# The expert phase of an attention and mixture-of-experts kernel: two tiles at a time instead of one

## What is computed

```python
x = x + xattn(layernorm(x), ctx, ctx, Wq, Wk, Wv, Wo, bo, mask)   # 32 batches x 256 tokens x 256, 16 heads of 64, causal
x = x + ffn(layernorm(x), router_w, router_b, weights1, bias1, weights2, bias2)

def ffn(x, ...):
    logits = x_flat @ router_w.T + router_b          # 8192 tokens, 32 experts
    routed_idx = argmax(logits)
    h = relu(x_flat @ w1[e] + b1[e])                 # 256 -> 64
    y = relu(h @ w2[e] + b2[e])                      # 64 -> 256
    # each token takes the y of its own expert
```

## Time and profile before

| what | us |
|---|---|
| median of 3 runs | 1811.64 (1810.61 to 1812.76) |
| the profiled execution, own time | 1811.58 |
| its span, first to last instruction | 1809.8 |
| TensorE busy in the span | 1753.6 |
| VectorE, ScalarE, POOL busy | 1247.4, 1033.9, 282.4 |

### The profile page before, as it was taken

One profiled execution on the slowest core, in us unless ns is written; L12 is line 12 of the kernel. 1 busy time (PEld: TensorE's weight loads), 2 busy tenths in 40 slices (PEclk: granted clock), 3 DMA queues, 4 the chain that ended last, 5 costly groups with the idle time before them and its releaser, 6 DMA issues. The chain is left out here.

```text
span 1809.8 us, 42548 instructions
## 1 busy us (share of the span) xinstructions
PE 1753.6 (97%) x12580; PEld 1356.3 (75%) x12581; DVE 1247.4 (69%) x5361; ACT 1033.9 (57%) x3206; POOL 282.4 (16%) x377
## 2 busy tenths in 40 slices
PE   5999999999999999999999999999999996899997
PEld 4777788778877887777877788788778874566664
DVE  5677777777777777777777777777777776233332
ACT  4656666666666666666666666666666663343442
POOL 1011011111111111111111111111101111233333
PEclk9999999999999999999999999999999998555555
DMA  7830000000000000000000000000000000333321
GB/s 209 237 99 21 24 24 24 22 21 24 24 24 24 24 24 24 24 24 24 20 22 24 24 24 24 24 24 24 24 24 18 18 12 16 90 101 101 86 70 24
DMA packets 70009, 77.61 MB, mean 43 GB/s; under 512 B 11703, under 2 KB 64093, under 8 KB 69985
## 3 DMA queue, kind: packets, MB, share of 16 engines
q1 hardware_dynamic: 61778, 60.18, 11.9%
q0 software_dynamic: 7680, 16.93, 2.6%
q10 hardware_dynamic: 528, 0.22, 0.0%
HBM read 47.60 MB, written 33.88 MB: 45 GB/s over the span
## 5 line engine op out<-in xcount | busy, mean ns | idle before, releaser
L672 ACT ACTIVATE Sm<-Sm,mneg 128x128 f32<-128x128 f32 (+1 forms) x1024 | 455.5, 448 | 366.9 <-DVE mneg L904 366.1
L904 DVE CUSTOM_DVE_ANT_0 Sm<-psS,MK 128x128 f32<-128x128 f32 (+1 forms) x1024 | 304.4, 353 | 123.7 <-PE psS L519 114.0
L546 PE MATMUL psO<-PT,V 128*64 128x256 f32 x2048 | 277.5, 392 | 2.3 <-ACT PT L665 2.0
L519 PE MATMUL psS<-KT,QT 64*128 64x128 f32 (+1 forms) x2048 | 238.5, 351 | 4.4 <-DVE mneg L904 2.6
L530 PEld LDWEIGHTS psT<-ident,Sm 128*128 128x128 f32 x1536 | 163.7, 141 | 98.7 <-issue 98.1
L530 PE MATMUL psT<-ident,Sm 128*128 128x128 f32 x1536 | 224.6, 282 | 0.0
L546 PEld LDWEIGHTS psO<-PT,V 128*64 128x64 f32 x2048 | 124.3, 136 | 123.8 <-issue 74.6
L665 ACT ACTIVATE PT<-psT 128x768 f32<-128x768 f32 x256 | 205.5, 803 | 6.6 <-PE psT L530 2.5
L672 ACT ACTIVATION_READ_ACCUMULATOR Sm<-Sm,mneg 128x1 f32 x1024 | 195.1, 191 | 0.0
L921 DVE TENSOR_TENSOR Sm<-Sm,rinv 128x512 f32<-128x512 f32 x256 | 192.8, 753 | 0.0
L519 PEld LDWEIGHTS psS<-KT,QT 64*128 64x128 f32 x2048 | 134.9, 187 | 59.7 <-issue 44.3
(11 more groups left out here) (151 smaller groups left out, 3229.8 us busy)
## 6 DMA issues: line engine op xcount, KB each, us to landing
lists<-pad SPq DMA_DIRECT2D x8, 1560.0 KB, 16.4
XS<-lists SPq DMA_DIRECT2D x96, 130.0 KB, 2.1
x_in<-in_x SPq DMA_DIRECT2D x32, 256.0 KB, 2.7
ctx_in<-in_ctx SPq DMA_DIRECT2D x32, 256.0 KB, 2.7
xr<-in_x SPq DMA_DIRECT2D x32, 256.0 KB, 2.7
W2R<-in_L_ffn_weights SPq DMA_DIRECT2D x1, 2048.0 KB
out<-Y,tok POOLq DMA_INDIRECT x96, 2.6
W2R<-in_L_xattn_Wq SPq DMA_DIRECT2D x1, 1024.0 KB, 10.1
```

Of the source, the lines that this page charges most:

```text
L519: last = nc.tensor.matmul(psS[:, side, o:o + (it + 1) * P], QT[rows, p, it * P:(it + 1) * P], KT[rows, p, 0:(it + 1) * P], start=True, sto ...
L546: last = nc.tensor.matmul(psO[DH * side:DH * side + DH, 0:N], V[:, t, DH * h:DH * h + DH], PT[:, side, cols], start=(t == 0), stop=(t == 1))
L672: nc.scalar.activation(v, v, ACT.Exp, bias=mneg[:, p % 2, k:k + 1], scale=-1.0, accum_out=rsum[:, p % 2, k:k + 1]).then_inc(s_exp, 1)
L904: nc.vector.tensor_tensor_reduce(out=Sm[:, p % 4, side, cols], in0=psS[:, side, cols], in1=MK[:, cols], scale=-SCALE, scalar=3e38, op0=ALU ...
```

## The change

The expert phase works on pairs of tiles. There are `NP` = 48 pairs (`NET` stays 96) and eight buffers for pairs. One load brings both tiles. The buffers, PSUM tiles and semaphore steps hold a pair: four transposes, then the W1 products of the two tiles alternately, one into PSUM partitions 0 to 63 and one into 64 to 127, then two W2 products. VectorE normalises twice and adds once per pair; ScalarE copies W1 for the first tile of the pair and VectorE for the second. The bias comes from a table `B1T`, transposed twice over (so `b1` is loaded into two halves), and is no longer a column of `W1R`; the ReLU is one instruction for each tile, with an index load of its own. SyncE waits with the next load of a buffer for the addition that has read it (`s_y`), not for the stores; VectorE waits for the stores of the buffer's last use before it writes `tok` and `Y` anew. The token numbers are copied at the addition, not at the norm. On VectorE the memsets of `HT` come after the table row.

```diff
-    NET = -(-(NT + E - 1) // U) * U
+    NP = B * N // P // 2 + E // 2
+    NET = 2 * NP
...
-            act.dma_start(b1_in[:], b1).then_inc(s_small, 16)
+            for half in range(2):
+                act.dma_start(b1_in[:, half, :], b1).then_inc(s_small, 16)
...
-            nc.vector.memset(W1R[HID:P, :, KD * HID], 0.0)
             dve.wait_ge(s_b1_pe, 1)
-            nc.vector.tensor_copy(W1R[0:HID, :, KD * HID], psS[0:HID, 1, 0:E]).then_inc(s_b1r, 1)
+            nc.vector.tensor_copy(B1T[:], psS[:, 1, 0:E]).then_inc(s_b1r, 1)
...
-        psXT = [psS[:, u, :] for u in range(2)]
-        psH = [psT[:, u, :] for u in range(2)]
-        psY = [psO, psW]
+        psXT = [psO, psW]
+        psH = psR
+        psY = [psS, psT]
...
+                        for t in range(2):
+                            nc.gpsimd.indirect_dma_start(out_rows, bass.IndirectOffsetOnAxis(ap=tok[u][:, t:t + 1], axis=0),
+                                                         Y[u][:, t, :], None, bounds_check=last_token, oob_is_err=False
+                                                         ).then_inc(s_done[u], 16)
...
-                        wait_apart(sp, s_passed, s_done[u], 16 * i)
+                        wait_apart(sp, s_passed, s_y, U * (i - 1) + u + 1)
                         load(i, u)
...
+                def norm_pair(i, u):
                     dve.wait_ge(s_in[u], 16 * i + 16)
+                    for t in range(2):
+                        last = nc.vector.tensor_scalar(XH[u][:, t, :], XS[u][:, t, 0:D], XS[u][:, t, D:D + 1],
+                                                       XS[u][:, t, D + 1:D + 2], ALU.subtract, ALU.mult)
+                    last.then_inc(s_xh, 1)
+
+                def add_pair(i, u, free):
+
+                    if free:
+                        wait_apart(dve, s_passed, s_done[u], 32 * i)
+                    nc.vector.tensor_copy(tok[u][:], XS[u][:, :, D + 2])
                     dve.wait_ge(s_y_pe, U * i + u + 1)
+                    nc.vector.scalar_tensor_tensor(out=Y[u][:], in0=psY[u % 2][:, :, 0:D], scalar=0.0,
+                                                   in1=XS[u][:, :, 0:D], op0=ALU.max, op1=ALU.add).then_inc(s_y, 1)
+
+                def w1_copy(i, u):
+                    e = expert(dve, U * i + u, 1)
+                    nc.vector.tensor_copy(W1[u][:, 1, :], W1R[:, bass.ds(e, 1), :].rearrange("p a c -> p (a c)")
+                                          ).then_inc(s_w1[1], 1)
...
                 def hidden(i, u):
+                    e = [expert(act, U * i + u, t) for t in range(2)]
                     act.wait_ge(s_h_pe, U * i + u + 1)
+                    for t in range(2):
+                        last = nc.scalar.activation(HT[u][0:HID, t, :], psH[u % 2][half(t), 0:P], ACT.Relu,
+                                                    bias=B1T[half(t), bass.ds(e[t], 1)])
+                    last.then_inc(s_h, 1)
...
                     for c in range(KD):
-                        last = nc.tensor.matmul(psH[u % 2][0:HID, 0:P], W1[u][:, c * HID:(c + 1) * HID],
-                                                XHT[u][:, c, :], start=(c == 0), stop=(c == KD - 1))
+                        for t in range(2):
+                            last = nc.tensor.matmul(psH[u % 2][half(t), 0:P], W1[u][:, t, c * HID:(c + 1) * HID], XHT[u][:, t, c, :],
+                                                    start=(c == 0), stop=(c == KD - 1))
                     last.then_inc(s_h_pe, 1)
...
                 def y_of(i, u, free=True):
-                    e = pe.value_load(tile_row[0:1, bass.ds(U * i + u, 1)], min_val=0, max_val=E - 1)
-                    pe.wait_ge(s_h, U * i + u + 1)
+                    e = [expert(pe, U * i + u, t) for t in range(2)]
                     if free:
                         pe.wait_ge(s_y, U * i + u - 1)
+                    pe.wait_ge(s_h, U * i + u + 1)
+                    for t in range(2):
+                        last = nc.tensor.matmul(psY[u % 2][:, t, 0:D], HT[u][:, t, :],
+                                                W2R[0:HID + 1, bass.ds(e[t], 1), :].rearrange("p a d -> p (a d)"),
+                                                start=True, stop=True)
+                    last.then_inc(s_y_pe, 1)
```

More of the change, by code:

```diff
@@ L1016, in attention_moe @@
         tile_row = kept("tile_row", [1, P], I32)
[L1017 to L1023, removed]
+        XS = [kept(f"XS{u}", [P, 2, ROW]) for u in range(U)]
+        XH = [kept(f"XH{u}", [P, 2, D]) for u in range(U)]
+        W1 = [kept(f"W1_{u}", [P, 2, KD * HID]) for u in range(U)]
+        XHT = [kept(f"XHT{u}", [P, 2, KD, P]) for u in range(U)]
+        HT = [kept(f"HT{u}", [HID + 1, 2, P]) for u in range(U)]
+        Y = [kept(f"Y{u}", [P, 2, D]) for u in range(U)]
+        tok = [kept(f"tok{u}", [P, 2], I32) for u in range(U)]
         s_ht1 = sem("ht_ones")
@@ L1029, in attention_moe @@
         s_in = [sem(f"tile_in{u}") for u in range(U)]
-        s_w1 = sem("w1_copied")
+        s_w1 = [sem(f"w1_copied{t}") for t in range(2)]
         s_xh = sem("xh_ready")
@@ L1038, in attention_moe, with expert, half @@
         s_done = [sem(f"tile_out{u}") for u in range(U)]
-        psXT = [psS[:, u, :] for u in range(2)]
-        psH = [psT[:, u, :] for u in range(2)]
-        psY = [psO, psW]
+        psXT = [psO, psW]
+        psH = psR
+        psY = [psS, psT]
         out_rows = out.rearrange("b n d -> (b n) d")
+        def expert(eng, j, t):
+            return eng.value_load(tile_row[0:1, bass.ds(2 * j + t, 1)], min_val=0, max_val=E - 1)
+        def half(t):
+            return slice(HID * t, HID * t + HID)
         with nc.Block() as block2:
@@ L1065, in load @@
                 def load(i, u):
-                    sp.dma_start(XS[u][:], lists[bass.ds((U * i + u) * P, P), :]).then_inc(s_in[u], 16)
+                    sp.dma_start(XS[u][:], lists[bass.ds((U * i + u) * 2 * P, 2 * P), :].rearrange("(t p) r -> p t r", p=P)
+                                 ).then_inc(s_in[u], 16)
                 for u in range(U):
                     load(0, u)
-                with sp.Fori(1, NET // U) as i:
+                with sp.Fori(1, NP // U) as i:
                     for u in range(U):
-                        wait_apart(sp, s_passed, s_done[u], 16 * i)
+                        wait_apart(sp, s_passed, s_y, U * (i - 1) + u + 1)
                         load(i, u)
                 for u in range(U):
-                    sp.wait_ge(s_done[u], 16 * (NET // U))
+                    sp.wait_ge(s_done[u], 32 * (NP // U))
             @block2.vector
             def _(dve):
-                for u in range(U):
-                    last = nc.vector.memset(HT[u][HID:HID + 1, :], 1.0)
-                last.then_inc(s_ht1, 1)
                 dve.wait_ge(s_te_pe, 1)
@@ new lines, in w1_copy @@
+                def w1_copy(i, u):
+                    e = expert(dve, U * i + u, 1)
+                    nc.vector.tensor_copy(W1[u][:, 1, :], W1R[:, bass.ds(e, 1), :].rearrange("p a c -> p (a c)")
+                                          ).then_inc(s_w1[1], 1)
+                AHEAD = 3
+                for u in range(U):
+                    last = nc.vector.memset(HT[u][HID:HID + 1, :, :], 1.0)
+                last.then_inc(s_ht1, 1)
+                dve.wait_ge(s_row, 1)
+                dve.wait_ge(s_w1r, 16)
@@ L1112, in _ @@
-                with dve.Fori(0, NET // U - 1) as i:
-                    tiles_of(i, True)
-                tiles_of(NET // U - 1, False)
+                            norm_pair(i + 1, u + AHEAD - U)
+                            w1_copy(i + 1, u + AHEAD - U)
+                        add_pair(i, u, free)
+                pairs_of(0, False, True)
+                with dve.Fori(1, NP // U - 1) as i:
+                    pairs_of(i, True, True)
+                pairs_of(NP // U - 1, True, False)
             @block2.scalar
@@ L1139, in _, with pairs_of @@
                     xht(0, u)
-                def tiles_of(i, more):
+                def pairs_of(i, more):
                     for u in range(U):
@@ L1148, in tiles_of @@
                                 f(i + 1, u + 2 - U)
-                with act.Fori(0, NET // U - 1) as i:
-                    tiles_of(i, True)
-                tiles_of(NET // U - 1, False)
+                with act.Fori(0, NP // U - 1) as i:
+                    pairs_of(i, True)
+                pairs_of(NP // U - 1, False)
             @block2.tensor
@@ L1163, in turn @@
                         pe.wait_ge(s_xht, U * i + u - 1)
-                    xh = XH[u][:].rearrange("p (d c) -> p c d", c=KD)
-                    for c in range(KD):
-                        last = nc.tensor.transpose(psXT[u % 2][:, c * P:(c + 1) * P], xh[:, c, :], ident[:])
+                    for t in range(2):
+                        xh = XH[u][:, t, :].rearrange("p (d c) -> p c d", c=KD)
+                        for c in range(KD):
+                            o = (t * KD + c) * P
```

(7 more changed lines are left out.)

56 lines of the change are left out of this document (23 added, 33 removed).

## The result

The changed kernel took 1746.32 us (median of 4, 1745.55 to 1747.73), against 1811.91 for the kernel before measured beside it: a ratio of 0.9639 [0.9623, 0.9656], 65.6 us less. Measured twice more, the same kernel took 1689.68 us once (0.9324 [0.9309, 0.934]) and 1746.32 us the other time (0.9631 [0.9608, 0.9655]). Each measurement kept to its level: 4, 4 and 6 executions, with nothing in between. What separates them is the clock. All times are medians; among the experiments one execution of e1 (3915 us) and one of e10 (3115 us) were slow without a profile that shows why, and without them the two medians would be 0.1 and 0.4 us lower.

What follows compares the result with a forecast made beforehand. TensorE at half clock bounds the expert phase, 2.63 us per tile. First W2 at 1553.7, 4 pairs at 3.91 and 43 at 2.75 reach 1687.6, the end 1699.9, 109.9 less: 1702 us; range 1690 to 1754.

Steps and rivals of the forecast that it cites:

- the first rival: TensorE's clock stays at 0.50 through the expert phase: 1749 us (1743 to 1754), chance 0.37.
- Half clock: TensorE in the expert phase at clock 0.50: 3.91 us per pair against 5.25 before.
- W1 halves side by side: Eight W1 matmuls on two PSUM halves run together: 1.05 us per pair; otherwise 0.85 more.
- The clock rises: TensorE's clock goes from 0.50 to 1.00 some 10 to 30 us into the expert phase; chance 0.53.
- And keeps the clock: TensorE in the expert phase, at 2.2 us per pair, stays at full clock as in the attention phase.
- POOL binds at full clock: POOL's two descriptor jobs set the expert phase's pair at 2.75 us, ScalarE's 2.5 close behind.
- The four pairs at 3.91: Start of the expert phase: 4 pairs at 3.91 us, then 43 at 2.75, together 133.9 us.
- VectorE's copy beside POOL: VectorE's W1 copy, 0.2 us, could be added to POOL's period if they block one another: +9 us.
- Loads behind the addition, the prologue: Loads waiting for the addition: nothing; one more b1 issue before the phase: nothing, or 1 to 2 us without cover.
- The second: W1 halves run one after the other at low clock, 41 us more: 1790 us, chance 0.05.
- the third: Each pair's second store on POOL holds additions and the chain: 1848 us at 3.0 per job, chance 0.02.
- fourth: Nothing gained: TensorE's exposed index loads plus W1 matmuls in line give 5.25 us per pair: 1811 us, chance 0.03.

Runs made afterwards that it cites:

- e1: Changed kernel with HT filled with zeros up to 128 rows, so the W2 product runs over all rows: 1692.56 us, ratio 0.9342.
- e10: Changed kernel with W2 on 128 rows, the zeros and ones of HT written by POOL instead of VectorE: 1732.34 us, ratio 0.9541.
- e5: Changed kernel with loads waiting for stores and TensorE paused once before round 1, W2 product on 65 rows: 1745.64 us, ratio 0.9636.
- after: Changed kernel, unmodified, first measurement, beside the kernel before: 1746.32 us, ratio 0.9639.
- e2: Kernel before the change, one tile at a time, with only HT filled with zeros to 128 rows: 1712.45 us, ratio 0.9453.
- e6: Changed kernel with loads waiting for stores and TensorE paused once before round 1, W2 product on 128 rows: 1700.49 us, ratio 0.9386.
- e9: As e5, but both tiles' W1 products one after the other in PSUM partitions 0 to 63: 1743.24 us, ratio 0.9619.
- after_again: Changed kernel, unmodified, measured a second time: 1689.68 us, ratio 0.9324.
- after_third: Changed kernel, unmodified, measured a third time with six executions: 1746.32 us, ratio 0.9631.
- e4: Changed kernel, but SyncE's loads wait for the buffer's stores as before the change: 1688.55 us, ratio 0.9319.
- e8: Changed kernel without the store of each pair's second tile, half of the output rows unwritten: 1673.18 us, ratio 0.9232.

## Why the prediction was right, and where it was not

The range of 1690 to 1754 was wide enough for both levels of the clock, and that is why it holds. The single forecast, 1702, was met by no measurement: the first lies 44 us above it, at the time of the first rival, to which 0.37 was given, and the one at full clock lies 12 us below it, 0.3 us outside of the forecast's own 1690 to 1724.

**Half clock.** The sum held: 3.91 us per pair was forecast and 3.91 measured; the first W2 product was forecast at 1553.7 and came at 1554.21; 1747.7 was forecast for the rival's span and 1746.0 measured. The last W2 product came at 1731.30 instead of 1734.6, since the first pairs ran at full clock (2.11 us from the first to the second) and the stall gave only part of it back. The span came out right in part by luck: from that product to the end it was 14.7 us instead of 13.1, since the last four stores queue on POOL.

**W1 halves side by side.** Right: x8 in 1.12 us against 1.97 in line at half clock, 0.66 against 1.09 at full. That the whole kernel gains 41 us by it at half clock was not isolated.

**The clock rises.** It did, but by luck and not by the reason given. The prediction had the steady order raise it, 10 to 30 us into the phase. It rose at 1553.8, behind work of the entry that holds no W2 product yet; the steady order at 65 rows did not raise it in 152 us (e5) nor in the 161 us from 1564 to 1725 (after). By the Trainium skill, "TensorE: Matmul & The Clock Gate", Part 4, transposes would have kept it down; the rise follows a stretch of transposes and W1 products alone, in which transposes fill 2.9 of the 4.3 us from 1549.52 to 1553.8, and e2 and e6 hold 1.00 with transposes in every tile, so these traces do not bear the rule out. The W1 product on all columns, which the prediction counted for the rise, is not what decides: with it and 65 rows the clock stayed down (e5), with the W1 products in line on half of the columns it came back (e9). The rows of the W2 product, which it named as what was still against a rise, are what decides between e5 and e6.

**"And keeps the clock".** This step failed in two of three measurements. It took what the attention phase bears as proof for this phase. The runs show a clock at 65 rows that holds as long as nothing happens (after_again, 116 us) and doesn't come back once lost (e5, after and after_third, to the end). The two levels lie 1746 - 1690 = 56 us apart; e5 against e4, where the pause is put in by the edit, 57 us.

**POOL binds at full clock.** Right (e8), but mis-sized. I took 2.75 us per pair; the stores start 1.28 apart, 2.56 per pair: 43 x 0.19 = 8 us. The four pairs at 3.91 were not there: 4 x 1.35 = 5 us more. Of these 13.6 us the span shows 11.4 (1699.9 against 1688.5). And the place of the limit was another. I let the additions wait for POOL, with the last W2 product at 1687.6. It came at 1668.93; the buffers let TensorE run ahead, and POOL has its queue to finish:

```profile
1668.93 1.26 PE L1217 MATMUL psT<-W2R,HT 65*128 x4 [0.56 <-issue]
...
1670.23 0.69 DVE L1107 SCALAR_TENSOR_TENSOR Y<-psT,XS 128x512 f32<-128x512 f32 x1 [1.06 <-PE psT L1217]
...
1679.38 0.97 POOL L1063 DMA_INDIRECT out<-Y,tok  x1 [0.30 <-issue]
```

From the last addition to the last store it is 9.15 us of stores alone, and then 9.1 to the end, as forecast.

**VectorE's copy beside POOL.** By the Trainium skill, "SBUF — State Buffer", section "Who interferes with whom", the copy, in a two-port mode, and GpSimd would block one another, which the prediction put at +9 us. The traces hardly show it: in after_again 31 of the 48 copies of W1 lie beside a POOL job in time, and 29 of them take the usual 0.22 us; two take 0.45 and 0.46, as does the one at 1558.75 shown above. The POOL jobs stay at 0.97 and 1.28 apart, so it costs the period nothing.

**Loads behind the addition, the prologue.** Nothing, as forecast: e4 against after_again 0.1%; in the first profile loads hold up VectorE for 1.0 us in all. Of the prologue no cost shows: the first matmul of the expert phase starts at 1544.27 in the kernel before and between 1542.9 and 1545.4 in the profiles of the changed one and its variants.

**Rivals.** The second (1790) is out by the 1.12 us of the eight W1 matmuls, the third (1848) and fourth (1811) by the time. The first came in two of three measurements; 0.53 to 0.37 for the clock was too sure of the wrong question, whether it rises, where it should have asked what happens when TensorE misses work for some 3 us.

**Open: the stall.** VectorE and ScalarE, the two engines beside TensorE that load the tile's expert into a register, stop for some 3 us and go on together. It is in the profiles of after, after_third, e9 and e10, and not in the other nine (after_again, e1 to e8). It isn't the wait for loads alone (after_again has it unchanged, without a stall; e9, whose loads wait for the stores, has stalls), nor the chip alone (e8 ran without, e9 with, on one chip). That the stall made the clock fall is read from the order of events; no run took the stall out and left the rest. One sign goes with it. SyncE's load issues last 367 ns or more in eight of the nine (332 in e2, which loads single tiles); in the four with stalls some are recorded far shorter:

```profile
L1074 SPq DMA_DIRECT2D XS<-lists x48: 18/373/936, 1545.4 to 1706.0; - x48
```

The kernel before has such short records too (down to 5 ns) and no such stall, so this is no proof of anything. No run here tells the cause.

## What to carry to other kernels

When a phase sits at half clock with TensorE always busy, look at how many rows its products contract over: filling 65 rows up to 128 with zeros gave the kernel before 99 us, and its price in the changed kernel was some 3 us (e1 against after_again, 1692.56 and 1689.68), where e1's expectation put the zeros at 2.2. Where a clock once lost doesn't come back, a kernel can have two times, and the runs of one measurement don't show it: measure again, in another group, before an edit is credited with the difference (e4's 58 us were nothing). And before TensorE is made faster, read the start-to-start distance of the engine with the fixed price per job; its queue can set the end even where nobody waits for it.

## What the runs showed of the hardware that was not expected

- The rise and the fall of the clock ask for different things: a stream with the W2 product on 65 rows held 1.00 for 116 us (after_again) and, after one stall, stayed at 0.50 to the end, with TensorE busy without a gap from 1564 to 1725 (after). With 128 rows it came back 4.9 us after TensorE went on (e6).
- A stall of VectorE and ScalarE together, some 3 us in the changed kernel, for which the profile names no instruction of the core; the additions lost 43.7 us to it in e10, nothing in nine other profiles.
- An indirect store of 128 rows occupies POOL for 0.97 us, and back to back two of them start 1.28 apart, at either clock of TensorE.
